# The bucket attention of a three-layer kernel, rewritten as a stage of its own with packed score and value matmuls

## What is computed

```python
h = _ln(x, ln1_g, ln1_b)
qkv = h @ w_qkv + b_qkv
q, k, v = jnp.split(qkv, 3, axis=-1)
qb, kb, vb = (buck(q), buck(k), buck(v))                       # B, nb, 64, 16, 16
kp = jnp.concatenate([jnp.zeros_like(kb[:, :1]), kb[:, :-1]], axis=1)
vp = jnp.concatenate([jnp.zeros_like(vb[:, :1]), vb[:, :-1]], axis=1)
kc = jnp.concatenate([kp, kb], axis=2)                         # the bucket before, and its own
vc = jnp.concatenate([vp, vb], axis=2)
scores = jnp.einsum('bnihd,bnjhd->bnhij', qb, kc) * scale
mask = (j < BUCKET) | (j - BUCKET <= i)
attn = jax.nn.softmax(jnp.where(mask, scores, -jnp.inf), axis=-1)
ob = jnp.einsum('bnhij,bnjhd->bnihd', attn, vc).reshape(B, T, C)
x = x + ob @ w_out + b_out
```

## Time and profile before

| | |
|---|---|
| runs | 4908.69, 4929.43, 4920.05 us; median 4920.05 |
| the profiled execution | 4908.69 us, its span 4908.8 us |
| PE busy in the span | 4331.1 us (88%) |
| DVE, ACT, POOL busy | 2249.6, 1413.8, 1258.3 us |
| the stage's loop | 1690 to 2575 us |

### The profile page before, as it was taken

One profiled execution on the slowest core, in us unless ns is written; L12 is line 12 of the kernel. 1 busy time (PEld: TensorE's weight loads), 2 busy tenths in 40 slices (PEclk: granted clock), 3 DMA queues, 4 the chain that ended last, 5 costly groups with the idle time before them and its releaser, 6 DMA issues. The chain is left out here.

```text
span 4908.8 us, 71554 instructions
## 1 busy us (share of the span) xinstructions
PE 4331.1 (88%) x23249; PEld 2982.9 (61%) x23250; DVE 2249.6 (46%) x5734; ACT 1413.8 (29%) x4622; POOL 1258.3 (26%) x1134
## 2 busy tenths in 40 slices
PE   4999999994996499999998989999687899996875
PEld 3676777762664377777775656676343466764442
DVE  4555555552555334333331156666223466664223
ACT  1333333331111222222222234444111244442111
POOL 2333333333223311111111033343101233432000
PEclk9999999996998578777779989999888999998887
DMA  3000000004001200000001010000100000001003
GB/s 102 2 1 2 1 1 1 2 1 154 30 30 64 89 1 1 1 1 1 1 1 55 17 35 6 9 6 6 55 12 9 28 6 9 6 6 52 12 11 104
DMA packets 102500, 115.02 MB, mean 23 GB/s; under 512 B 11384, under 2 KB 92428, under 8 KB 101516
## 3 DMA queue, kind: packets, MB, share of 16 engines
q1 hardware_dynamic: 97292, 98.38, 6.0%
q0 software_dynamic: 4992, 13.64, 0.8%
HBM read 66.91 MB, written 27.26 MB: 19 GB/s over the span
## 5 line engine op out<-in xcount | busy, mean ns | idle before, releaser
L636 ACT ACTIVATE win_probs<-win_score,win_negmax 128x128 f32<-128x128 f32 (+2 forms) x1170 | 464.1, 405 | 1324.3 <-DVE win_negmax L766 1324.3
L396 POOL TENSOR_TENSOR win_probs<-win_probs,win_rsum 128x512 f32<-128x512 f32 (+1 forms) x420 | 422.7, 1007 | 1465.1 <-DVE win_rsum L781 771.7
L766 DVE TENSOR_REDUCE win_negmax<-win_score 128x2 f32<-128x512 f32 (+2 forms) x422 | 283.0, 671 | 945.5 <-PE win_score L522 479.2
L1498 PE MATMUL ffn_hidden<-ffn_hT,ffn_weights_w 128*128 128x512 f32 x640 | 321.0, 662 | 153.3 <-DVE ffn_inner L1590 151.4
L1779 PE MATMUL rot_lin<-rot_weights_w_qkv,rot_hT 128*128 128x512 f32 x816 | 404.9, 619 | 7.5 <-ACT rot_qk L1875 5.5
L1903 ACT ACTIVATE rot_probs<-rot_probs,rot_negmax 128x256 f32<-128x256 f32 x520 | 260.0, 501 | 366.6 <-DVE rot_negmax L1971 366.6
L1498 PEld LDWEIGHTS ffn_hidden<-ffn_hT,ffn_weights_w 128*128 128x128 f32 x640 | 133.7, 214 | 332.7 <-issue 169.8
L794 DVE COPY win_probsT<-win_turned 128x512 f32<-128x512 f32 (+1 forms) x416 | 276.2, 664 | 93.0 <-PE win_turned L532 92.5
L516 PE MATMUL win_score<-win_KT,win_QT 32*128 32x256 f32 x1036 | 294.4, 403 | 0.0
L1817 PE MATMUL rot_score<-rot_KT,rot_QT 64*128 64x256 f32 x1040 | 292.9, 406 | 0.0
L532 PE MATMUL win_turned<-keep_ident,win_probs 128*128 128x128 f32 x1600 | 287.8, 306 | 0.0
(11 more groups left out here) (271 smaller groups left out, 7912.4 us busy)
## 6 DMA issues: line engine op xcount, KB each, us to landing
weights_w<-in_L_ffn_W SPq DMA_DIRECT2D x16, 512.0 KB
scratch_rows_in<-keep_xn SPq DMA_DIRECT2D x1, 5120.0 KB, 16.5
experts_rows<-scratch_rows_in SPq DMA_DIRECT2D x40, 128.0 KB, 2.0
scratch_rows_out<-experts_y POOLq DMA_DIRECT2D x40, 128.0 KB, 2.0
rot_weights_w_qkv<-in_L_ffn_wqkv SPq DMA_DIRECT2D x3, 1536.0 KB, 6.5
rot_h<-keep_xn SPq DMA_DIRECT2D x36, 128.0 KB
rot_h<-keep_xn SPq DMA_DIRECT2D x36, 127.0 KB
keep_xn<-in_L_attn_x SPq DMA_DIRECT2D x4, 1024.0 KB, 9.4
```

The lines of the kernel that those rows point to most:

```text
L396: pool.tensor_tensor(mine, mine, bcast(rsum[:, u % 4, 0:heads], [P, heads, keys]), ALU.mult)\
L636: last = act.activation(probs[:, u % 4, i * width:(i + 1) * width], score[u % 4][:, i * width:(i + 1) * width], ACT.Exp, bias=negmax[:, u ...
L766: dve.tensor_reduce(negmax[:, u % 4, 0:heads], score[u % 4][:, 0:heads * keys].rearrange("p (h k) -> p h k", h=heads), AX.X, ALU.max, nega ...
L1498: last = pe.matmul(hidden[m % RING][k][:], w1[:, c, a:a + P], hT[:, c, :], start=(c == 0), stop=(c == KC - 1))
```

## The change

Layer 1 gets a function of its own, `bucket_attention`; `window_attention` serves layer 0 as before. What differs from the stage before:

- Scores are made for two units at once, after their two masks. For each head one matmul has the first bucket's 64 queries as weights and one the second's, both over 128 keys and both with 32x64 weights. The two units alternate, on other partitions and into other banks.
- For that the tiles of KT lie in reversed order (`k_slot`), so that the tile before comes behind the own one, and one strided operand covers the own first half and the second half of the tile before. The last slot repeats the first for the next step.
- `weigh` is done once a tile for all four units, with the units innermost; `probsT` has four buffers for that and `po` two halves.
- V is written once by DVE, both parities by one instruction into a padded layout. POOL makes `V_first` from it, with a product (by `going` or one) and a copy on 64 partitions each, and drains between.
- The input is turned one tile further ahead (hT, n + 3), and the order on each engine is written out per tile. The matmul that cleared `po` (430) is gone.

```diff
+def bucket_attention(nc, io, keep, following):
+    UNITS = 4
+    HEADS_PER = HEADS // UNITS
+    U = UNITS * TPG
+    HALF = P // 2
+    prologue = [("hT", 0), ("QK", 0), ("V", 0), ("hT", 1), ("QK", 1), ("V", 1), ("hT", 2)]
+    per_tile = [("QK", 2), ("V", 2), ("out", -1), ("hT", 3)]
+    order = [(name, n + ahead) for n in range(TPG) for name, ahead in per_tile]
+    by_dve = ("QK", "V", "out")
+    first_bank = lambda i: (i - len(prologue)) % 2
+    dve_before = sum(name in by_dve for name, _ in prologue)
+    act_before = len(prologue) - dve_before
+    k_slot = lambda m: TPG - 1 - m % TPG
+    v_slot = lambda m: m % TPG
+    VW = D + HD
...
+                def share_values(g, m, v_taken):
+                    kept = keep.going[HALF:P, bass.ds(g + m // TPG + 1, 1)] if v_slot(m) == TPG - 1 else one[HALF:P, :]
+                    pool.drain()
+                    pool.wait_ge(*v_taken)
+                    pool.tensor_tensor(V_first[HALF:P, v_slot(m + 1), :], V[HALF:P, v_slot(m), :],
+                                       kept.to_broadcast([HALF, 2 * VW]), ALU.mult)
+                    pool.drain()
+                    pool.tensor_copy(V_first[0:HALF, v_slot(m), :], V[0:HALF, v_slot(m), :])
+                    pool.drain()
+                    pool.sem_inc(first_ready.sem, 1)
...
+                with pool.Fori(0, NG) as g:
+                    for n in range(TPG):
+                        w = n * UNITS
+                        divide(g, w + 3)
+                        prepare(g, n + 3)
+                        divide(g, w + 4)
+                        share_values(g, n + 2, taken(g, order.index(("V", n + 2))))
+                        divide(g, w + 5)
+                        divide(g, w + 6)
...
+                def linear_step(it, name, n):
+                    i = order.index((name, n))
+                    pe.wait_ge(*taken(it, i - 2))
+                    if name == "QK":
+                        pe.wait_ge(*taken(it, i - 1))
+                    linear_work(it, name, n, lin_banks[i % 2])
+                def scores(it, v):
+                    n, pair = divmod(v, 2)
+                    pe.wait_ge(exp_done.sem, exp_done.at(it, 2 * v - 2))
+                    if v > 1 and pair == 0:
+                        pe.wait_ge(*taken(it, order.index(("QK", n)) if n > 1 else -2))
+                    js = (2 * pair, 2 * pair + 1)
+                    for j in js:
+                        pe.matmul(score[j][:], keep.identb[:], mask[:].unsqueeze(1).to_broadcast([P, HEADS_PER, P]),
+                                  start=True, stop=False)
+                    cur = k_slot(n) * P
+                    for i in range(HEADS_PER):
+                        c, odd = divmod(i, 2)
+                        for j in js:
+                            rows = slice(32 * j, 32 * j + 32)
+                            q, k = QT[rows, n % 2, c, :], KT[rows, odd, c, :]
+                            first = k[:, cur:cur + 2 * P].rearrange("p (a b) -> p a b", b=HALF)[:, 0:TPG:3, :]
+                            pe.matmul(score[j][0:HALF, i * P:(i + 1) * P], q[:, 0:HALF], first,
+                                      start=False, stop=(i == HEADS_PER - 1))
+                            last = pe.matmul(score[j][HALF:P, i * P:(i + 1) * P], q[:, HALF:P], k[:, cur:cur + P],
+                                             start=False, stop=(i == HEADS_PER - 1))
+                    last.then_inc(scores_ready.sem, 1)
+                def turn(it, w):
+                    pe.wait_ge(probs_ready.sem, probs_ready.at(it, w + 1))
+                    pe.wait_ge(probsT_ready.sem, probsT_ready.at(it, w))
+                    for i in range(HEADS_PER):
+                        last = pe.transpose(turned[:, i * P:(i + 1) * P], probs[:, w % UNITS, i * P:(i + 1) * P], keep.ident[:])
+                    last.then_inc(turned_ready.sem, 1)
+                def weigh(it, n):
+                    pe.wait_ge(probsT_ready.sem, probsT_ready.at(it, (n + 1) * UNITS))
+                    pe.wait_ge(first_ready.sem, first_ready.at(it, n))
+                    for c in range(KC):
+                        for half in range(2):
+                            values = V if half else V_first
+                            for odd in range(2):
+                                a, q = odd * D + c * P, (2 * c + odd) * P + half * HALF
+                                to = n % 2 * D + c * P + half * HALF
+                                for j in range(UNITS):
+                                    last = pe.matmul(po[32 * j:32 * j + 32, to:to + HALF],
+                                                     values[:, v_slot(n), a + 32 * j:a + 32 * j + 32],
+                                                     probsT[:, j, q:q + HALF], start=(odd == 0), stop=(odd == 1))
+                    last.then_inc(pv_done.sem, 1)
...
+                    if name == "QK" and n == 0:
+                        pe.wait_ge(*prologue_taken(i))
+                        scores(0, 0)
+                        scores(0, 1)
+                pe.wait_ge(*prologue_taken(len(prologue) - 1))
+                with pe.Fori(0, NG) as g:
+                    for n in range(TPG):
+                        scores(g, 2 * n + 2)
+                        weigh(g, n - 1)
+                        turn(g, n * UNITS)
+                        linear_step(g, "QK", n + 2)
+                        turn(g, n * UNITS + 1)
+                        linear_step(g, "V", n + 2)
+                        scores(g, 2 * n + 3)
+                        turn(g, n * UNITS + 2)
+                        linear_step(g, "out", n - 1)
+                        turn(g, n * UNITS + 3)
+                        linear_step(g, "hT", n + 3)
...
+                with act.Fori(0, NG) as g:
+                    for n in range(TPG):
+                        w = (n + 1) * UNITS
+                        softmax(g, w)
+                        take_output(g, n - 1)
+                        softmax(g, w + 1)
+                        softmax(g, w + 2)
+                        softmax(g, w + 3)
+                        i = order.index(("hT", n + 3))
+                        act.wait_ge(lin_ready.sem, lin_ready.at(g, i + 1))
+                        take_turned_h(lin_banks[i % 2])
...
+                    if k_slot(n) == 0:
+                        dve.drain()
+                        last = dve.tensor_scalar(KT[:, :, :, TPG * P:], KT[:, :, :, 0:P],
+                                                 keep.going[:, bass.ds(g + n // TPG + 1, 1)], None, ALU.mult)
+                    last.then_inc(dve_took.sem, 1)
+                def take_values(n, lin):
+                    apart = V[:, v_slot(n), :].rearrange("p (odd x) -> p odd x", odd=2)[:, :, 0:D]
+                    apart = apart.rearrange("p odd (h e) -> p odd h e", e=2 * HD)[:, :, :, 0:HD]
+                    by_parity = lambda t: t.rearrange("p (h odd d) -> p odd h d", odd=2, d=HD)
+                    dve.tensor_tensor(apart, by_parity(lin[:, 0:D]), by_parity(b_v[:]), ALU.add).then_inc(dve_took.sem, 1)
...
+                with dve.Fori(0, NG) as g:
+                    for n in range(TPG):
+                        w = n * UNITS
+                        maxima(g, w + 4)
+                        maxima(g, w + 5)
+                        invert(g, w + 3)
+                        take_turned(g, w)
+                        take_queries_keys(g, n + 2, wait_linear(g, "QK", n + 2))
+                        take_turned(g, w + 1)
+                        invert(g, w + 4)
+                        take_values(n + 2, wait_linear(g, "V", n + 2))
+                        maxima(g, w + 6)
+                        maxima(g, w + 7)
+                        invert(g, w + 5)
+                        take_turned(g, w + 2)
+                        take_out(g, n - 1, wait_linear(g, "out", n - 1))
+                        take_turned(g, w + 3)
+                        invert(g, w + 6)
...
-                window_attention(nc, io, keep, 1, mlp)
+                bucket_attention(nc, io, keep, mlp)
```

216 lines of the change are left out of this document (added).

## The result

The changed kernel takes 4377.8 us (median of 4 runs, 4373.1 to 4383.9) against 4921.7 for the kernel before (4 runs): 0.8905 of the time, 95% interval 0.8889 to 0.8920, 544 us less. The forecast was 4578, in a range from 4470 to 4700.

The account below looks back on a forecast made before the run. PE was taken to bound the rewritten stage; its new tile of 14 us (upper clock) and 22.1 (lower), at today's clock share, made 17.0, 10.7 less, times 32 = 342 us saved: 4578 us, range 4470 to 4700.

Parts of the forecast that it names:

- PE bounds the stage, and DVE's copies are late next: Rewritten stage's loop: PE sets the time, others wait; then turns wait for DVE's copy, about 0.8 us idle each.
- Prices of the old tile: Old loop tile: 21.7 us at the upper clock, 38.2 at the lower, 27.4 mixed, against 27.7 seen.
- Scores: New tile's score matmuls: 2.1 to 4.2 us for 9.9 at the upper clock; 3.0 taken, 5.0 at the lower.
- Sums: New tile's 64 weighted-sum matmuls: 1.3 us for 4.0 at the upper clock, 2.5 for 7.4 at the lower.
- What stays: Masks, transposes and projections of a tile: 7.7 us at the upper clock, 14.6 at the lower.
- PE's waits: PE waiting for DVE in the new tile: 14 us taken instead of 12.0 at the upper clock, none at the lower.
- With the clock's share as now: Stage's loop keeps 0.52 of the time at the upper clock: 17.0 us a tile, 342 us saved in all.
- rival 3: Denser stream holds the upper clock throughout: 14 us a tile, 438 us saved, 4482; chance 0.17.
- rival 2: PE idles each tile for DVE and the clock stays low: 22.1 us a tile, 179 saved, 4741; chance 0.12.
- rival 1: Matmul count, not streaming, sets PE's time: 19.9 us a tile, 250 us saved, 4670; chance 0.15.
- rival 4: Slower: each change of array tile costs a drain, about 0.2 us at 128 instructions a tile, 5397 us; chance 0.04.
- POOL's copies hidden: POOL's V_first copies, about 1.1 us each, delay divisions needed only next tile; at most 2 us a tile otherwise.

Follow-up runs that it names:

- grouped run: The kernel before with each unit's four 128-query score matmuls first, then its eight of 64 queries; 4664.6 us, ratio 0.9484.
- shape run: The kernel before with keys in reversed tile order and two 32x64-weight matmuls over 128 columns a head in place of three; 4528.4 us, ratio 0.9208.

## Why the prediction was wrong

- **PE bounds the stage, and DVE's copies are late next**: right. PE showed 90%, and its named waits are the two predicted ones.
- **Prices of the old tile**: the total was right, its split not. I put the 0.4 us of a head in which nothing streams on two changes of shape at 0.2 each. The grouped run shows 0.14 a change; the rest is that two matmuls with 128-column weights come every 0.11 us, not every 0.056. The sum did not suffer from it, since the new scores have neither.
- **Scores**: the concurrent bound was the true one. I took 3.0 us a tile; 2 x 1.03 = 2.1 measured, the cheap bound. Four parts of the array do work at once, two row groups among them.
- **Sums**: 1.3 taken, 1.03 measured with the gap, all four column groups at once.
- **What stays**: 7.7 taken, 6.7 measured, and this I had not questioned. A turn takes 0.44 to 0.49 us (0.59 before), a mask 0.26 (0.31), QK 1.79 (1.89), V 0.86 (0.97): the new order puts work of one weight shape side by side, so presumably fewer changes of shape are paid around it.
- **PE's waits**: 2 us added, 1.1 measured. With the three terms above, the tile at the upper clock is 11.06 us where I had 14, 94 us over 32 tiles.
- **"With the clock's share as now"**: this is the step that failed. The sum kept 0.52 of the time at the upper clock, and the loop ran at 1.00. At my own 14 us a tile, that would have given 14.0 in place of 17.0, 96 us over 32 tiles. That was rival 3, at 0.17, and even it (4482) lies above the measured 4378, because I had tied my own upper-clock price to it; the two errors, 96 and 94 us, are nearly the whole of the 200. The shape run shows why the share could not be carried over: the clock followed the same score stretches that the change removes. I had written that reason down against rival 2 and not used it in the sum.
- **The range** left out the joint case. Each lower bound was in the text (12.5 us a tile at the upper clock; the clock at 1.00), but they were never combined: 4920 - (27.7 - 12.5) x 32 = 4434. Even that is 56 us above the measured median, since the 7.7 us of what stays had no cheap bound.
- **Rivals 1, 2 and 4**: matmul count does not set the time (16 ns a matmul in the sums), the clock did not stay down, and a change of tile within a shape shows no price (starts 0.01 us apart).
- **POOL's copies hidden**: right: none of PE's waits names them. DVE's relief, which my sum gave no price, was worth 27 us.
- **"No DMA moves"**: the sum had nothing for PE's stops. The loop's instruction transfers fell from 70 to 5, and the seven stops with 13.5 us went with them.

The 544 us, by the runs: 389 for one score shape with 128-column operands, clock and stops included; 59 for the new order of the stage; 92 for the packed sums and units together (68 and 29 when each is undone alone). The 4 left are the difference between two medians of the kernel before (4921.7 and 4917.3).

## What to carry to other kernels

When a change removes the very stretches around which the clock fell, do not carry the old clock share into the new sum; price both levels, and combine the bounds. Before packing matmuls, look at the mix of weight shapes: sorting the same matmuls by shape gave 250 us here without touching the data. Look for idle time that the profile puts down to "issue" at the start of each loop step, and at the instruction transfers beside it. And once PE is no longer alone as the bound, the order of the copies that free its only bank is worth a look: 36 us for four moved lines.

## What was not expected of the hardware

- PE takes matmuls past ones that wait for a busy part of the array: with the units in turn, the second unit still started beside the first, and only 29 of the 61 us forecast were lost.
- A change between weight shapes cost 0.12 to 0.14 us (128x128 and 32x64, 32x128 and 32x64), and eight of them a unit left the clock at 1.00 where the score weights were narrow.
- With 128-column f32 weights a 64-column matmul came every 0.11 to 0.13 us at the upper clock and every 0.23 us at the lower.
- The granted clock went with the mix of matmuls, with PE busy for about 98% of the time or more: means of 0.69, 0.76 and 1.00 were seen in this stage with the same scores computed. The 0.95 and 0.98 of two more runs come from stretches behind stops of PE of about 3 us, one for each loop step.
